# VectorE makes every addition of the softmax denominators in two attentions

## The chip, the cores and the metric

The kernel runs on one core of a Trainium2 chip. The metric is the time of one execution on the device in microseconds, as the median of several runs. The engines of the core run side by side, each with its own in-order queue, and meet at semaphores: TensorE (PE; its weight loads are PEld), VectorE (DVE), ScalarE (ACT), GpSimd (POOL) and SyncE (SP), which starts most of the transfers.

## What is computed

The reference is a residual network of four layers, each a cross-attention and a mixture of experts, on x of 2 x 512 x 256 with a context of 2 x 1024 x 256. The change touches the attentions of layers 0 and 1. Layer 0 has 16 heads of 64, keys and values from the context, and clips the scores; layer 1 has 8 heads of 64, keys and values from the context and from the latents themselves (1024 + 512 keys here), with no clip.

```python
# layer 0
attn = jnp.einsum('bhnd,bhsd->bhns', q, k) * scale
attn = jnp.clip(attn, -11.0, 11.0)
attn = jax.nn.softmax(attn, axis=-1)
out = jnp.einsum('bhns,bhsd->bhnd', attn, v)
# layer 1
k = jnp.concatenate([k_x, k_l], axis=2)
v = jnp.concatenate([v_x, v_l], axis=2)
sim = jnp.einsum('bhid,bhjd->bhij', q, k)
attn = jax.nn.softmax(sim, axis=-1)
out = jnp.einsum('bhij,bhjd->bhid', attn, v)
```

## The kernel before

One function writes the queue of each engine. An attention goes in steps; one step is one pair of heads of one batch entry: 16 steps in layer 0, 8 in layer 1 (`self.steps` in `Plan64`). In a step, `attend` runs over nk tiles of 128 keys, kt = 0 to nk - 1; nk is 8 in layer 0 and 12 in layer 1. For one tile:

- TensorE makes the scores of both heads, keys down and 512 queries across, into two banks of a ring of four (lines 661 and 662, in layer 1 also 664, which adds the negated row maximum).
- ScalarE takes the exponential of both, out of the banks, into a tile of 128 x 1024 (`slot`, line 948). Tile 0 of a step goes to an accumulator `SA`, of which there are two in turn; the others go to a ring of three buffers `PT`. A buffer is written again when tile kt - 3 was both weighted and added.
- In layer 0 VectorE clips the exponentials between exp(-11) and exp(11), in place (line 814).
- Two tiles later TensorE multiplies the tile with the values (`weigh`, line 646) into bank 4.
- The denominator: for kt = 1 to nk - 1 the tile is added to `SA` elementwise, 128 x 1024, in place. In `Plan64` a table `adds` says which engine makes which addition: VectorE those with kt % 4 == 3 (line 807), GpSimd the others (line 1009). Each waits for the one before it. Both engines issue add(kt - 2) in the iteration of tile kt, behind the clip of tile kt on VectorE, and the last two, add(nk - 2) and add(nk - 1), after the last tile's side work.

Between tiles a generator of side work is advanced by a number of turns worked out ahead (`paced`): first `divide` of the step before (line 680 on TensorE sums `SA` over the partitions with a matrix of ones and waits for the last addition; line 824 takes the reciprocal, line 827 multiplies bank 4 by it), then parts of `prepare` of the next step: projections of keys (line 275, `mm3`), the rotation (744 on VectorE, the sum 979 on GpSimd), the split of the keys into two parts (872 on ScalarE, 728 on VectorE), `output` (692, 837), values (572, 880, 884), and at the end the projection of the queries, which ScalarE places (907) and VectorE splits (765). The first scores of the next step wait for these (`placed`). In layer 1 the row maxima follow: line 624 makes scores for them, VectorE reduces them one by one (785), then over the parts with a negation (790), and ScalarE spreads that on a diagonal (925), for which the next step's scores wait. Every second step VectorE also splits the next weights (720), after ScalarE (866). What is left of the side work once the tiles are through is run before the next step; on VectorE that is behind the last two additions.

TensorE's `divide` stands in its queue behind the scores of the next step's tile 0, and ahead of the next key projection. In the last step of an attention there is nothing to prepare, and the side work is over after tile 0.

Of the kernel before, what the change touches and what calls it, by code (L numbers as in the profile page):

```python
# [33 lines left out]
class Semaphores(dict):  # L34


    def __init__(self, nc, ctx):
        super().__init__()
        self.nc, self.ctx = nc, ctx
# [105 lines left out]
def paced(weights, total, shares):  # L145

    out, done, i = [], 0.0, 0
    for share in shares:
        n = 0
        while done < share * total - 1e-6 and i < len(weights):  # L150
            done += weights[i]
            i += 1
            n += 1
        out.append(n)
    return out
# [6 lines left out]
class Kernel:  # L162
# [74 lines left out]
    def view(self, off, cnt, pat=None, **kw):  # L237
        v = self.AF[:, off:off + cnt]
        return v.rearrange(pat, **kw) if pat else v

    def rview(self, off, cnt, pat=None, **kw):
        v = self.AR[:, off:off + cnt]
        return v.rearrange(pat, **kw) if pat else v

    def pair(self, off, cnt, pat=None, **kw):
        return self.rview(off, cnt, pat, **kw), self.rview(off + cnt, cnt, pat, **kw)
# [226 lines left out]
class Plan64:  # L473


    def __init__(self, K, layer):
        self.own = layer == 1
        self.layer = layer
        S = 1536 if self.own else 1024
        self.nk = nk = S // P  # L480
        rview, view, pair = K.rview, K.view, K.pair
        self.KT = [rview(6144 + 3072 * i, 2 * S, "p (h n) -> p h n", h=2) for i in range(2)]
        self.QA = [rview(12288 + 2048 * i, 1024, "p (h n) -> p h n", h=2) for i in range(2)]
        self.QB = [rview(13312 + 2048 * i, 1024, "p (h n) -> p h n", h=2) for i in range(2)]
        self.DG = [rview(16384 + 1024 * i, 1024, "p (h n) -> p h n", h=2) for i in range(2)]
        self.PT = [view(5120 + 1024 * i, 1024, "p (h n) -> p h n", h=2) for i in range(3)]
        self.VA = [view(8192 + 1536 * i, nk * 128, "p (t c) -> p t c", c=128) for i in range(2)]
        self.OT, self.VT = view(11264, 512), view(11776, 512)
        self.COS, self.SIN = K.TB[:, 0:1024], K.TB[:, 1024:2048]
        self.W = [pair(4096, 1024), pair(18432, 1024)]  # L490
        self.SA = [view(15616 + 1024 * i, 1024, "p (h n) -> p h n", h=2) for i in range(2)]
        self.TM = [view(2048 + 1024 * i, 1024, "p (h n) -> p h n", h=2) for i in range(2)]
        self.npair = 4 if self.own else 8
        self.steps = [(p, b) for p in range(self.npair) for b in range(B)]
        self.n = len(self.steps)
        prep = [1.3] * 4 + [1.3, 0.4, 1.3, 0.4] + [1.3]
        if self.own:
            prep += [1.3, 1.3, 0.4] + [0.85] * 24 + [0.0]
        total = sum(prep) + 1.5
        shares = [(kt + 1) / nk for kt in range(nk)]  # L500
        self.pace = []
        for n in range(self.n):
            ahead = prep if n + 1 < self.n else [0.0, 0.0]
            weights = [0.5] * (n > 0) + ahead[:2] + [1.0] * (n > 0) + ahead[2:]
            self.pace.append(paced(weights, total, shares))

        self.k_lo = 6 if self.own else 4
        self.nv = 3 if self.own else 2

        self.adds, made = {}, K.adds_made  # L510
        for n in range(self.n):
            for kt in range(1, nk):
                who = "sum_vector" if kt % 4 == 3 else "sum_gpsimd"
                made[who] += 1
                self.adds[n, kt] = who, made[who]

# [195 lines left out]
def vector_attention64(v, K, A, bases):  # L712
    own, nk = A.own, A.nk
    wv0, ex0, o0 = (bases[x] for x in ("weighed", "exp", "out"))
# [84 lines left out]
    def add(n, kt):  # L799
        if kt < 1 or A.adds[n, kt][0] != "sum_vector":  # L800
            return
        if kt > 1:
            v.wait_ge(*A.adds[n, kt - 1])
        v.wait_ge("exp", ex0 + 2 * (n * nk + kt + 1))
        if not own:
            v.wait_ge("clip", bases["clip"] + n * nk + kt + 1)
        v.e.tensor_tensor(A.SA[n % 2], A.SA[n % 2], A.slot(n, kt), ALU.add).then_inc(*v.up("sum_vector"))  # L807

    def attend(n, side):
        for kt in range(nk):  # L810
            if not own:
                pt = A.slot(n, kt)
                v.wait_ge("exp", ex0 + 2 * (n * nk + kt + 1))
                v.e.tensor_scalar(pt, pt, CLIP_LO, CLIP_HI, ALU.max, ALU.min).then_inc(*v.up("clip"))  # L814
            add(n, kt - 2)
            run(side, A.pace[n][kt])
        add(n, nk - 2)
        add(n, nk - 1)
# [1828 lines left out]
```

## Time and profile before

| | |
|---|---|
| Time, median of 3 runs | 2950.0 us (2949.27 to 2957.69) |
| The profiled execution | 2951.47 us |
| Its span | 2949.7 us |
| Mean granted clock of TensorE | 0.883 |
| Busy, share of the span | PE 81%, PEld 57%, DVE 53%, ACT 31%, POOL 32% |
| First attention, steps | 90 to 605 us of the span |
| Second attention, steps | 910 to 1364 us |

The busy time of an engine counts what it executes, not what it waits for. A time in brackets behind an instruction of the timeline is the idle time of its engine ahead of it, with what ended it. The granted clock is 1.00 at 2.4 GHz and 0.50 at 1.2 GHz.

### The profile page before, as it was taken

The numbers are of one execution on the slowest core, as the hardware profiler recorded it, in microseconds if no ns is written. First come the engines' busy times: TensorE is split into PE (matmuls) and PEld (weight loads), VectorE is DVE, ScalarE is ACT, GpSimd is POOL, SyncE is SP. The second block draws the span as 40 slices with busy tenths as digits, with TensorE's granted clock in tenths as the row PEclk, the third lists the DMA queues.
The fourth block names the chain that finished last, engine by engine and source line by source line (L and its number), as shares of the span: only waits on it lengthen the run. The fifth ranks groups of instructions, "written<-read, shape, count | busy, mean of one in ns | idle before, by whom it ended". The sixth has DMA issues, their size and how long they took to land.

```text
span 2949.7 us, 31683 instructions
## 1 busy us (share of the span) xinstructions
PE 2375.2 (81%) x11832; PEld 1668.5 (57%) x11832; DVE 1576.8 (53%) x2705; ACT 907.5 (31%) x1752; POOL 948.3 (32%) x817
## 2 busy tenths in 40 slices
PE   3799999848968999996885777399788989659994
PEld 2455555528955555553874454289644444348884
DVE  5788888743145665653315766322477767421222
ACT  2454555412124444442112223000224444401111
POOL 2354554433332342333222211355400000044443
PEclk8899999959978999997897777599879999769997
DMA  3000000008930000000482321199522221048883
GB/s 119 1 9 10 18 10 10 1 33 310 316 128 1 0 10 9 1 1 15 157 273 71 80 65 50 48 318 327 164 57 69 59 62 45 17 170 298 300 296 116
DMA packets 103178, 298.08 MB, mean 101 GB/s; under 512 B 16913, under 2 KB 45841, under 8 KB 102641
## 3 DMA queue, kind: packets, MB, share of 16 engines
q0 software_dynamic: 45168, 206.99, 20.3%
q1 hardware_dynamic: 57856, 89.07, 10.2%
q8 instruction: 94, 1.54, 0.2%
q14 instruction: 60, 0.48, 0.1%
HBM read 244.22 MB, written 20.32 MB: 90 GB/s over the span
## 4 chain that ended last, share of the span: by engine, by line
PE 41%; DVE 12%; issue 7%; DMA 4%; POOL 2%; ACT 2%; SPq 0%; another core or an unknown queue 0%; DVEq 0%; POOLq 0%; ACTq 0%
PE psum L1860 8%; PE psum L275 7%; PE psum L1883 6%; PE psum L1211 3%; DVE plain L1363 3%; PE psum L1224 2%; PE psum L646 2%; DMA plain<-in_l_en,plain 2%; PE psum L1184 2%; PE psum L661 2%; DVE plain L1381 2%; DMA plain<-sorted_x 2%; DVE plain L1360 1%; PE psum L1250 1%; PE psum L664 1%
## 5 line engine op out<-in xcount | busy, mean ns | idle before, releaser
L275 PE MATMUL psum<-split 128*128 128x512 f32 (+1 forms) x1776 | 475.3, 416 | 57.1 <-DVE split L348 11.1
L1860 PE MATMUL psum<-plain 128*128 128x128 f32 x3904 | 494.4, 279 | 10.2 <-DMA plain<-in_l_shared 8.5
L1860 PEld LDWEIGHTS psum<-plain 128*128 128x128 f32 x3904 | 486.3, 196 | 22.3 <-issue 10.5
L275 PEld LDWEIGHTS psum<-split 128*128 128x128 f32 x1776 | 337.0, 208 | 191.8 <-issue 95.7
L1009 POOL TENSOR_TENSOR plain<-plain 128x1024 f32<-128x1024 f32 x144 | 363.5, 2524 | 239.8 <-DVE plain L807 195.9
L1984 POOL DMA_INDIRECT plain<-in_l_ffn,plain x274 | 259.8, 948 | 401.7 <-PE psum L1883 378.7
L948 ACT ACTIVATE plain<-psum 128x512 f32<-128x512 f32 x448 | 251.4, 595 | 310.5 <-PE psum L664 145.2
L1883 PE MATMUL psum<-plain 128*128 128x256 f32 x1160 | 304.2, 385 | 28.0 <-DVE plain L1949 25.5
L1480 ACT ACTIVATE plain<-psum 128x512 f32<-128x512 f32 (+3 forms) x384 | 185.8, 542 | 228.7 <-PE psum L1224 227.6
L646 PE MATMUL psum<-plain 128*64 128x512 f32 x896 | 236.9, 616 | 5.6 <-DVE plain L814 5.6
L1949 DVE TENSOR_TENSOR plain<-plain,psum 128x256 f32<-128x256 f32 x198 | 81.7, 419 | 298.2 <-ACT plain L1908 266.5
L1184 PE MATMUL psum<-split 128*128 128x512 f32 (+3 forms) x384 | 171.8, 517 | 75.6 <-DVE plain L1381 29.9
L1883 PEld LDWEIGHTS psum<-plain 128*128 128x128 f32 x1160 | 199.9, 192 | 49.9 <-DVE plain L1949 25.5
L1908 ACT ACTIVATE plain<-psum 128x256 f32<-128x256 f32 x198 | 75.8, 384 | 491.2 <-PE psum L1860 461.8
L661 PE MATMUL psum<-split 128*128 128x512 f32 x448 | 186.2, 416 | 39.2 <-issue 20.1
L662 PE MATMUL psum<-split 128*128 128x512 f32 x448 | 178.3, 398 | 0.0
L313 PE MATMUL psum<-plain 128*128 128x128 f32 x224 | 48.8, 395 | 157.4 <-DVE plain L303 121.1
L1363 DVE TENSOR_REDUCE plain<-psum 128x1 f32<-128x512 f32 x256 | 159.2, 684 | 29.0 <-PE psum L1184 28.4
L1184 PEld LDWEIGHTS psum<-split 128*128 128x128 f32 x384 | 87.1, 230 | 148.2 <-DVE plain L1363 47.6
L979 POOL TENSOR_TENSOR plain<-plain 128x512 f32<-128x512 f32 x44 | 60.7, 1380 | 342.1 <-DVE plain L744 312.7
L814 DVE TENSOR_SCALAR plain<-plain 128x1024 f32<-128x1024 f32 x128 | 136.1, 1063 | 57.6 <-ACT plain L948 57.0
L728 DVE TENSOR_TENSOR split<-plain,split 64x512 fp32r<-64x512 f32 x96 | 143.4, 1494 | 30.7 <-ACT split L872 27.4
(177 smaller groups left out, 3024.7 us busy)
## 6 DMA issues: line engine op xcount, KB each, us to landing
split<-split SPq DMA_DIRECT2D x288, 64.0 KB, 2.0
split<-split SPq DMA_DIRECT2D x96, 128.0 KB, 2.4
plain<-sorted_x SPq DMA_DIRECT2D x76, 128.0 KB
sorted_y<-plain SPq DMA_DIRECT2D x76, 128.0 KB
plain<-in_l_w SPq DMA_DIRECT2D x16, 512.0 KB
plain<-in_l_w SPq DMA_DIRECT2D x12, 640.0 KB, 3.8
plain<-in_l_ffn,plain POOLq DMA_INDIRECT x274
plain<-in_ctx SPq DMA_DIRECT2D x8, 512.0 KB, 6.1
```

The lines of the kernel that those rows point to most:

```text
L275: m = t.e.matmul(out, lhs[x], rhs[y], start=(first and n == 0), stop=(last and n == 2), skip_group_check=skip)
L646: m = t.e.matmul(K.bank(4)[64 * h:64 * h + 64, :], A.VA[i][:, kt, 64 * h:64 * h + 64], pt[:, h, :], start=(kt == 0), stop=(kt == nk - 1))
L661: t.e.matmul(K.bank(b), kk, A.QA[i][:, h, :], start=True, stop=False)
L662: m = t.e.matmul(K.bank(b), kk, A.QB[i][:, h, :], start=False, stop=not own)
L948: s.e.activation(pt[:, h, :], K.where("scores", k), ACT.Exp, scale=0.125).then_inc(*s.up("exp"))
L1009: g.e.tensor_tensor(A.SA[n % 2], A.SA[n % 2], A.slot(n, kt), ALU.add).then_inc(*g.up("sum_gpsimd"))
L1184: t.e.matmul(K.bank(b)[:, 0:kn], A.QZ[:, j, 128 * q:128 * q + 128], A.KHL[0][:, 512 * u:512 * u + kn], start=True, stop=True).then_inc(*t. ...
L1363: v.e.tensor_reduce(A.MXC[:, q, u:u + 1], s, AX.X, ALU.max).then_inc(*v.up("row_max", L, n, j, q, u))
L1480: s.e.activation(pt[:, j % 2, q0:512], K.bank(K.at.get(("scores", L, n, kt, j), 0))[:, q0:512], ACT.Exp, scale=0.25).then_inc(*s.up("exp", ...
L1860: m = t.e.matmul(K.bank(b)[:, 256 * z + P * f:256 * z + P * f + P], ws[:, f, c0:c0 + 128], xt[:, k, :], start=(f == 0 and k == 0 and z == ...
L1883: m = t.e.matmul(y, h[:, f, :], ws[:, f, A.cn - 256:A.cn], start=(u == 0 and f == 0), stop=(u == units - 1 and f == 1))
L1984: g.e.indirect_dma_start(A.W[A.slot(i)].rearrange("p f n -> p (f n)"), None, K.T[f"l{L}_ffn"], bass.IndirectOffsetOnAxis(K.WIX[:, j - A.ns ...
```

## The change

In `Plan64`, which plans both attentions, the table gives every addition to VectorE. The addition of tile 1 therefore is VectorE's now, and gets the wait that GpSimd's had: tile 0 lies in `SA`, and may be overwritten once it was weighted. Nothing else is changed: the place of each addition in the iteration is the same on both engines.

```diff
@@ -510,7 +510,7 @@
         self.adds, made = {}, K.adds_made
         for n in range(self.n):
             for kt in range(1, nk):
-                who = "sum_vector" if kt % 4 == 3 else "sum_gpsimd"
+                who = "sum_vector"
                 made[who] += 1
                 self.adds[n, kt] = who, made[who]
 
@@ -801,6 +801,9 @@
             return
         if kt > 1:
             v.wait_ge(*A.adds[n, kt - 1])
+        else:
+
+            v.wait_ge("weighed", wv0 + n * nk + 1)
         v.wait_ge("exp", ex0 + 2 * (n * nk + kt + 1))
         if not own:
             v.wait_ge("clip", bases["clip"] + n * nk + kt + 1)
```

## Rows read from the trace of the kernel before

**Rows 1.** Page's costliest groups: busy us, mean ns, idle before; then L807's durations.

```profile
L1009 POOL TENSOR_TENSOR plain<-plain 128x1024 f32<-128x1024 f32 x144 | 363.5, 2524 | 239.8 <-DVE plain L807 195.9
L814 DVE TENSOR_SCALAR plain<-plain 128x1024 f32<-128x1024 f32 x128 | 136.1, 1063 | 57.6 <-ACT plain L948 57.0
L728 DVE TENSOR_TENSOR split<-plain,split 64x512 fp32r<-64x512 f32 x96 | 143.4, 1494 | 30.7 <-ACT split L872 27.4
...
L807 DVE TENSOR_TENSOR plain<-plain x56: 1212/1222/1227, 113.4 to 1362.7; 128x1024 f32<-128x1024 f32 x56
...
L728 DVE TENSOR_TENSOR split<-plain,split x96: 685/689/2783, 38.2 to 1283.2; 64x512 fp32r<-64x512 f32 x96
```

**Rows 2.** Windows, two steps of the first attention: engines' busy us, granted clock.

```profile
187.48:219.64 32.16, 30.50 (x127) 17.36 (x126) 27.12 (x28) 16.98 (x29) 15.81 (x8) 1.00 0.00 1
219.64:251.48 31.84, 30.36 (x126) 17.35 (x126) 26.04 (x27) 15.92 (x28) 15.80 (x8) 1.00 0.06 21
```

**Rows 3.** Waits of TensorE, 100 to 550 us: total us, times, longest.

```profile
PE psum L661 <- issue: 18.7, 13, 1.4
PE psum L646 <- DVE plain L814: 3.0, 1, 3.0
```

**Rows 4.** Timeline across the end of one step: start, us, engine, line, [idle before].

```profile
216.03 2.13 DVE L814 TENSOR_SCALAR plain<-plain 128x1024 f32<-128x1024 f32 x1 [0.65 <-ACT plain L948]
...
217.80 2.44 ACT L907 ACTIVATE split<-psum 64x512 fp32r<-64x512 f32 x4 [1.81 <-PE psum L275]
...
220.28 0.69 DVE L765 TENSOR_TENSOR split<-psum,split 64x512 fp32r<-64x512 f32 x1 [0.55 <-ACT split L907]
221.00 1.23 DVE L807 TENSOR_TENSOR plain<-plain 128x1024 f32<-128x1024 f32 x1
...
221.07 0.47 PE L661 MATMUL psum<-split 128*128 128x512 f32 x1 [1.44 <-issue]
...
222.28 0.20 PEld L680 LDWEIGHTS psum<-plain 128*64 128x64 f32 x4 [0.48 <-DVE plain L807]
...
222.98 0.69 DVE L814 TENSOR_SCALAR plain<-plain 128x1024 f32<-128x1024 f32 x1 [0.76 <-ACT plain L948]
...
228.07 0.20 PEld L646 LDWEIGHTS psum<-plain 128*64 128x64 f32 x4 [0.35 <-DVE plain L827]
```

**Rows 5.** Timeline in the middle of two steps.

```profile
209.33 1.09 ACT L948 ACTIVATE plain<-psum 128x512 f32<-128x512 f32 x2 [0.88 <-POOL plain L1009]
...
232.02 2.94 DVE L728 TENSOR_TENSOR split<-plain,split 64x512 fp32r<-64x512 f32 x2 [0.29 <-ACT split L872]
```

**Rows 6.** Timeline at the end of the first attention's first step, VectorE and TensorE.

```profile
120.78 2.08 DVE L814 TENSOR_SCALAR plain<-plain 128x1024 f32<-128x1024 f32 x1 [0.41 <-ACT plain L948]
...
122.92 1.08 PE L646 MATMUL psum<-plain 128*64 128x512 f32 x4 [2.99 <-DVE plain L814]
123.92 0.70 PE L661 MATMUL psum<-split 128*128 128x512 f32 x1
...
127.63 1.65 PE L275 MATMUL psum<-split 128*128 128x512 f32 x6
```

**Rows 7.** Timeline in the first attention's last step.

```profile
589.09 1.36 DVE L814 TENSOR_SCALAR plain<-plain 128x1024 f32<-128x1024 f32 x1 [1.43 <-ACT plain L948]
...
603.71 1.23 DVE L807 TENSOR_TENSOR plain<-plain 128x1024 f32<-128x1024 f32 x1 [2.24 <-POOL plain L1009]
```

**Rows 8.** Timeline in the second attention: inside a step, and across its end.

```profile
1003.37 1.89 DVE L785 TENSOR_REDUCE plain<-psum 128x1 f32<-128x512 f32 x3 [1.41 <-PE psum L624]
...
1022.82 1.22 DVE L807 TENSOR_TENSOR plain<-plain 128x1024 f32<-128x1024 f32 x1
1023.95 0.16 DVE L790 TENSOR_REDUCE plain<-plain 128x4 f32<-128x12 f32 x1
...
1025.47 0.50 PE L661 MATMUL psum<-split 128*128 128x512 f32 x1 [2.16 <-ACT split L925]
```

**Rows 9.** Windows behind four of six such stalls: busy us, then the granted clock.

```profile
1025.40:1028.80 3.40, 3.33 (x13) 1.90 (x14) 0.61 (x1) 1.21 (x3) 0.00 (x0) 1.00 0.00 0
1086.60:1090.00 3.40, 3.40 (x9) 1.20 (x8) 0.97 (x1) 0.92 (x2) 0.00 (x0) 0.50 0.00 0
...
1265.80:1269.20 3.40, 3.40 (x13) 1.91 (x14) 0.69 (x1) 1.20 (x2) 0.00 (x0) 1.00 0.00 0
1325.50:1329.00 3.50, 2.17 (x5) 0.30 (x4) 1.28 (x1) 0.82 (x2) 0.00 (x0) 0.51 0.00 0
```

## What the change will do to the time

> **What bounds the kernel now.** Read the page first. The costliest group of GpSimd is the one the change removes, 144 additions of 2.52 us, and two groups of VectorE show a mean far above their shortest form: the clip L814 and the subtraction L728 [rows 1]. Then the busy time of two successive steps of the first attention: they take 32.16 and 31.84 us, TensorE is busy for 30.5 and 30.4 us of them at full clock, VectorE for 27.1 and 26.0, ScalarE and GpSimd for half [rows 2]. So TensorE sets the pace, VectorE is close behind. Then the waits of TensorE: in the stretch from 100 to 550 us nearly all its idle time is one stall of 1.44 us, once a step, ahead of the next step's first score matmul, and the profile names no releaser for it [rows 3]. The timeline names it [rows 4]: the query projection ends at 217.8, ScalarE places it in four pieces (L907, 2.44 us), VectorE subtracts (second L765, over at 220.97), and TensorE starts at 221.07. Anything that lengthens this chain, or adds a second stall to TensorE's in-order queue, is paid in full, 14 times (13 in that stretch, and once more at 573 us).
>
> **The change, part by part.** *Removed:* all 144 additions of GpSimd, 80 in the first attention (5 in each of 16 steps) and 64 in the second (8 in each of 8). *Added:* as many on VectorE, at 1.22 us, the time of its own additions of that shape, whose shortest and longest differ by 15 ns [rows 1]. That is 5 x 1.22 = 6.1 us a step in the first attention.
>
> *The relief.* Beside a GpSimd addition the clip takes 2.13 us, without one 0.69 [rows 4]; two L728 take 2.94 us beside one [rows 5], where the shortest of them takes 0.685 [rows 1]. With means of 1.06 and 1.49, eight clips and four L728 a step give back 8 x 0.37 + 4 x 0.80 = 6.2 us. VectorE's busy time stays where it is, 26 to 27 us a step. Which of these microseconds lie on the path decides the time, so I go by the order of the queues.
>
> *Inside a step.* VectorE's queue is clip(kt), add(kt-2), side work. The longest chain it makes: exp(kt) needs the buffer that add(kt-3) read, so exp, clip, add form a loop of 1.09 + 0.69 + 1.22 + about 0.05 = 3.05 us. Placed beside the trace of one step, exp(5) starts about 0.9 us earlier (GpSimd's add held it until 209.33 [rows 5]), exp(7) about 0.6 us later; the last clip, 1.44 us shorter, ends 0.8 us earlier, and add(5), queued ahead of the two L765, ends about 0.6 us before ScalarE has the first of them ready. The stall of 1.44 us stays: it hangs on L907, not on the adds or the clip. Cover left: 0.6 us. Nothing gained, nothing lost. The one new wait of VectorE, on the first weighting ahead of add(1), is for something done some 5 us earlier.
>
> *At the step's end.* add(6) and add(7) stand behind both L765. Before, GpSimd had done add(6) by then, and VectorE made only add(7), 221.00 to 222.23; L680, the matmul that sums over partitions, started at 222.28, already waiting for it [rows 4]. Now add(6) takes that place and add(7) follows, with 0.03 us for the wait on the one before. L680 starts 1.26 us later, and behind it in TensorE's queue stand the next projection and scores, with no slack before the next step's end. The reciprocal, the product and the first weighting at 228.07 move by no more than that [rows 4]. **14 x 1.26 = +17.6 us.** In every second step the weight split L720 follows the adds; it moves by the same 1.26 us and so does the projection that needs it.
>
> *The first of these transitions* is another case: TensorE waited 2.99 us for a clip of 2.08 us that now takes 0.69, and four scores and L680 ran at a lower clock, 3.71 us from 123.92 to 127.63 against the usual 2.22 [rows 6]. Clip at 121.47, three adds behind it (5, 6, 7) until 125.1, the split until 126.3, and the projection starts at 126.4 instead of 127.63. The reciprocal gains 0.9. I take **-1.0 us**.
>
> *The last step* has no side work after its first tile, and the loop of 3.05 us sets it. Clip 589.09 ends at 589.78 [rows 7], add(1) at 591.0, then exps every 3.05 us until 600.1, the last clip over at 601.9, three adds at 605.5. Before, the last addition, which waited for GpSimd, ended at 604.94 [rows 7]. **+0.6 us.**
>
> *The second attention.* Its steps are paced by the row maxima. In a tile VectorE is idle for 1.41 us between reductions [rows 8], and an add of 1.22 us without any wait fits in; cover left: 0.19 us a tile. If it didn't fit, TensorE would wait for a bank by the difference. At the step's end the negated maximum L790 is queued behind add(10) and add(11), of which GpSimd made the first: L807 at 1022.82, L790 at 1023.95, then ScalarE's L925, then TensorE after a stall of 2.16 us [rows 8]. One more add there: 6 x 1.25 = **+7.5 us** (of the seven transitions the first has its maximum ahead of the adds, and the last step waits for its exps).
>
> *TensorE's clock.* No row of before shows the longer stalls, so I bound them. Of the six stalls of 2.16 us, four were followed by some 3.4 us at half clock (1.2 GHz; granted 0.50, two rows of the four), two were not (1.00) [rows 9]; none of the fourteen of 1.44 us was (1.00 over both steps [rows 2]). The stall of 2.99 us was [rows 6]. The price of one is 3.71 - 2.22 = 1.5 us [rows 6]. In the second attention stalls grow to 3.4 us: I take six instead of four, 2 x 1.5 = +3.0 us. In the first attention a second stall of 1.26 us follows 1.2 us after that of 1.44: 2.7 us idle with work between. Between none and all 14 (0 to 21 us) I take four, nearer to the row of 1.44, as each stall alone is shorter than it: +6.0 us. The Trainium skill's "TensorE: Matmul & The Clock Gate" (The HAM clock gate) has just these two levels and says that idleness drops it; how much idleness in pieces is enough, these traces must tell.
>
> Sum: 17.6 - 1.0 + 0.6 + 7.5 + 3.0 + 6.0 = **+33.7 us** on the profiled execution's 2951.5 (its span of 2949.7 and 1.8 around it). The median of the runs is 2950.0, 1.5 below it: **2984 us**.
>
> **The rivals.** *A, forecast:* adds at the step's end are paid. *B, VectorE's busy time sets the time:* it is the busiest engine but TensorE and its busy time is left as it was, 6.1 added and 6.2 given back, so 2950 us. For it: the small margins. Against it: VectorE has 5 us of idle time a step, and the place of an instruction in its queue, not the sum, made L680 wait 0.48 us already [rows 4]. The Trainium skill's "Perfetto Trace Analysis" (Identifying the Most-Contended Engine) would look there, since it doesn't take matmul busy time as a measure; by that rule the change is neutral. *C, faster:* the step is paced by exps that GpSimd holds and clips that it stretches. If each step gained the 0.88 us of exp(5) [rows 5] and the 1.44 us of the last clip [rows 4], the first attention would gain 14 x (2.32 - 1.26) = 15 us; with the 7.5 us that the second attention costs that is 2943 us. It decides from the point at which L765 waits for VectorE and not for L907; the second L765 shows a wait of 0.55 us for L907 [rows 4], and the first one like it. The Trainium skill's "SBUF — State Buffer" (Who interferes with whom) lets a GpSimd instruction block VectorE for its whole length, and the 2.13 us agree, but it doesn't say that the path runs there. *D, far slower:* VectorE falls behind inside the step, its 0.6 us of cover gone. Each L765 later by x us adds 14x; with a late L979 or handoffs of 0.2 us in each turn of the loop x is 1: 2998 us, and all 14 drops of the clock in the first attention give 2999 by themselves.
>
> **How the numbers follow.** A 0.82, B 0.06, C 0.04, D 0.08. The lower end is the sum with no clock cost but for a missized first transition and last step: 2950 + 24.7 - 4 = 2970; the upper, eight or nine more drops of the clock at 1.5 us each, or part of D, 2997. Within 0.3% (what a measurement of this kernel can tell from no change) is 2941 to 2959. So C is the chance of faster, 0.04, B that of the same, 0.06, and A with D that of slower, 0.90.
>
> **What would show it.** L807 200 times at 1.22 us, no L1009; L814 near 0.7 us and L728 at 0.69; L680 2.5 us after a step's first score instead of 1.2; steps of 33.1 and 33.4 us; the stall ahead of it still 1.44 us; in the second attention stalls of 3.4 us. It is wrong if L680 doesn't wait for a second add, if L765 starts later than L907 allows, or if TensorE shows idle time in the middle of a step.

## The result

The changed kernel takes 2999.15 us (median of 4 runs, 2992.31 to 3003.92), the kernel before 2949.64 beside it: the ratio is 1.0161, with an interval of 1.0133 to 1.0189. That is 49.5 us slower, where 34 were forecast and 47 were the end of the range. A second measurement, below, gives 1.0158. The profiled execution is the slowest of the four, 3003.92 us with a span of 3002.2, so its time is 52.5 us over that of the profile of before.

The page after, its first line and three of its groups; they answer to [rows 1]:

```profile
PE 2395.7 (80%) x11832; PEld 1681.7 (56%) x11832; DVE 1629.4 (54%) x2849; ACT 907.0 (30%) x1752; POOL 583.2 (19%) x673
...
L810 DVE TENSOR_TENSOR plain<-plain 128x1024 f32<-128x1024 f32 x200 | 243.7, 1219 | 16.0 <-ACT plain L951 10.7
...
L982 POOL TENSOR_TENSOR plain<-plain 128x512 f32<-128x512 f32 x44 | 58.6, 1333 | 860.9 <-DVE plain L744 824.1
...
L817 DVE TENSOR_SCALAR plain<-plain 128x1024 f32<-128x1024 f32 x128 | 95.9, 749 | 85.3 <-ACT plain L951 84.8
```

GpSimd has lost 365 us of busy time, VectorE has gained 53: 144 additions of 1.22 us, less what its other instructions no longer lose to GpSimd. The clip, L817 now, went from a mean of 1.06 to 0.75 us. The subtraction L728 now never takes more than 0.69 us, as its line's own view shows (shortest, median, longest):

```profile
L728 DVE TENSOR_TENSOR split<-plain,split x96: 684/687/690, 38.9 to 1326.6; 64x512 fp32r<-64x512 f32 x96
```

The end of a step in the timeline after, against [rows 4]; behind each line in brackets is its engine's idle time and what ended it:

```profile
224.58 2.44 ACT L910 ACTIVATE split<-psum 64x512 fp32r<-64x512 f32 x4 [1.38 <-PE psum L275]
...
227.05 0.69 DVE L765 TENSOR_TENSOR split<-psum,split 64x512 fp32r<-64x512 f32 x1 [0.55 <-ACT split L910]
227.78 2.48 DVE L810 TENSOR_TENSOR plain<-plain 128x1024 f32<-128x1024 f32 x2
227.84 0.47 PE L661 MATMUL psum<-split 128*128 128x512 f32 x1 [1.44 <-issue]
...
230.31 1.08 PE L680 MATMUL psum<-plain 128*64 128x512 f32 x4 [1.30 <-DVE plain L810]
231.32 1.65 PE L275 MATMUL psum<-split 128*128 128x512 f32 x6
```

The stall of 1.44 us is where it was, with the same chain behind it. Two additions stand behind L765 instead of one, and L680 starts 2.47 us after the step's first score where it started 1.21 after it. In the second attention the stall ahead of a step's scores grew from 2.16 to 3.42 us, as two additions stand ahead of the negated maximum L790, against [rows 8]:

```profile
1056.93 2.47 DVE L810 TENSOR_TENSOR plain<-plain 128x1024 f32<-128x1024 f32 x2
1059.33 0.16 DVE L790 TENSOR_REDUCE plain<-plain 128x4 f32<-128x12 f32 x1
...
1060.85 0.76 PE L661 MATMUL psum<-split 128*128 128x512 f32 x1 [3.42 <-ACT split L928]
```

What differs most from the forecast is TensorE's clock. A drop means below that the granted clock falls from 1.00 (2.4 GHz) to 0.50 (1.2 GHz). Windows after, two steps of the first attention and then pieces of the first of them (busy us of PE, PEld, DVE, ACT, POOL, then the granted clock):

```profile
192.08:227.84 35.76, 33.02 (x126) 18.96 (x127) 27.76 (x33) 16.23 (x29) 2.55 (x2) 0.90 0.00 1
227.84:261.17 33.33, 30.51 (x126) 17.35 (x127) 25.94 (x32) 16.66 (x29) 2.86 (x2) 1.00 0.07 20
...
193.90:197.20 3.30, 2.65 (x6) 0.94 (x7) 2.96 (x4) 0.06 (x1) 0.00 (x0) 0.50 0.02 5
197.30:200.60 3.30, 3.30 (x9) 2.54 (x9) 3.27 (x3) 0.24 (x1) 0.00 (x0) 0.50 0.00 0
200.80:201.00 0.20, 0.20 (x2) 0.17 (x1) 0.20 (x1) 0.15 (x1) 0.00 (x0) 1.00 0.00 0
```

One step is at 2.4 GHz throughout and takes 33.3 us, as forecast. The other starts at 192.08, is at 1.2 GHz from some 194.0, before the end of the stall at L680, until 200.8, some 6.8 us, and takes 35.8 us. That is twice as long as behind the stall of 2.99 us in [rows 6], as these windows of before show:

```profile
120.50:124.00 3.50, 1.08 (x5) 0.27 (x5) 3.12 (x2) 1.30 (x2) 1.81 (x1) 1.00 0.00 0
124.10:127.40 3.30, 3.30 (x8) 1.19 (x8) 1.92 (x3) 1.19 (x2) 0.00 (x0) 0.50 0.02 5
127.50:130.00 2.50, 2.50 (x12) 1.99 (x11) 2.25 (x1) 0.14 (x1) 0.00 (x0) 1.00 0.00 0
```

Six of the thirteen steps between 157 and 603 us have a drop and are 34.9 to 35.9 us long; in five of them it lasts 6.8 us, in one, the shortest, 3.4. The other seven take 32.9 to 33.5 us.

### The profile page after: what moved, and what is told of

It is laid out like the page before. It is cut to its first block, busy times and chain, and to the rows that moved or that the text cites. A ratio compares the mean times of both kernels' runs of the same rounds, so it can differ in the third digit from the quotient of the medians.

```text
span 3002.2 us, 31683 instructions
## 1 busy us (share of the span) xinstructions
PE 2395.7 (80%) x11832; PEld 1681.7 (56%) x11832; DVE 1629.4 (54%) x2849; ACT 907.0 (30%) x1752; POOL 583.2 (19%) x673
## 3 DMA queue, kind: packets, MB, share of 16 engines
q0 software_dynamic: 45168, 206.99, 19.8%
q1 hardware_dynamic: 57856, 89.07, 10.1%
## 4 chain that ended last, share of the span: by engine, by line
PE 40%; DVE 13%; DMA 5%; issue 4%; POOL 3%; ACT 2%; SPq 0%; POOLq 0%; DVEq 0%; ACTq 0%
PE psum L1863 7%; PE psum L275 7%; PE psum L1886 5%; PE psum L1214 3%; DVE plain L1366 3%; PE psum L1227 2%; DMA plain<-in_l_en,plain 2%; PE psum L646 2%; PE psum L1187 2%; DVE plain L1384 2%; DMA plain<-sorted_x 2%; PE psum L661 1%; PE psum L1253 1%; DVE plain L1363 1%; PE psum L664 1%
## 5 line engine op out<-in xcount | busy, mean ns | idle before, releaser
L275 PE MATMUL psum<-split 128*128 128x512 f32 (+1 forms) x1776 | 484.9, 422 | 53.1 <-DVE split L348 11.1
L275 PEld LDWEIGHTS psum<-split 128*128 128x128 f32 x1776 | 344.3, 212 | 195.7 <-issue 96.0
L810 DVE TENSOR_TENSOR plain<-plain 128x1024 f32<-128x1024 f32 x200 | 243.7, 1219 | 16.0 <-ACT plain L951 10.7
L646 PE MATMUL psum<-plain 128*64 128x512 f32 x896 | 236.7, 615 | 4.6 <-DVE plain L817 4.6
L1187 PEld LDWEIGHTS psum<-split 128*128 128x128 f32 x384 | 87.5, 231 | 147.8 <-DVE plain L1366 47.6
L661 PEld LDWEIGHTS psum<-split 128*128 128x128 f32 x448 | 87.5, 195 | 102.7 <-issue 34.5
L817 DVE TENSOR_SCALAR plain<-plain 128x1024 f32<-128x1024 f32 x128 | 95.9, 749 | 85.3 <-ACT plain L951 84.8
```

What stands on the lines that cost most here:

```text
L275: m = t.e.matmul(out, lhs[x], rhs[y], start=(first and n == 0), stop=(last and n == 2), skip_group_check=skip)
L646: m = t.e.matmul(K.bank(4)[64 * h:64 * h + 64, :], A.VA[i][:, kt, 64 * h:64 * h + 64], pt[:, h, :], start=(kt == 0), stop=(kt == nk - 1))
L661: t.e.matmul(K.bank(b), kk, A.QA[i][:, h, :], start=True, stop=False)
L1187: t.e.matmul(K.bank(b)[:, 0:kn], A.QZ[:, j, 128 * q:128 * q + 128], A.KHL[0][:, 512 * u:512 * u + kn], start=True, stop=True).then_inc(*t. ...
```

## Experiments

All are measured against the kernel before on the same chip; it took 2957 to 2960 us there as a median, so ratios are compared, not microseconds.

To take the stages apart I use one pair of stretches in every profile. The first runs from the first reciprocal of the first attention (L824 before, L827 after) to the fifteenth, which are the 14 steps with the stall of 1.44 us; the second from the first to the seventh reciprocal of the second attention, 6 steps. Before, and then after:

```profile
127.76:575.86 448.10, 425.85 (x1764) 242.86 (x1764) 371.56 (x370) 229.43 (x398) 221.21 (x98) 1.00 0.03 9
969.90:1327.70 357.80, 332.47 (x1332) 194.30 (x1332) 219.09 (x284) 159.05 (x290) 131.69 (x60) 0.98 0.01 4
```

```profile
127.84:606.94 479.10, 439.65 (x1763) 251.06 (x1762) 374.30 (x441) 228.86 (x398) 38.20 (x28) 0.96 0.03 9
1004.00:1374.40 370.40, 337.53 (x1332) 196.60 (x1332) 252.05 (x332) 159.07 (x290) 15.29 (x12) 0.96 0.01 4
```

So 31.0 us of the 52.5 are in the first stretch and 12.6 in the second. VectorE's busy time in the first is 374.3 against 371.6 us: 70 more additions there cost it 2.7 us net.

### One attention at a time

```diff
-                who = "sum_vector"
+                who = "sum_vector" if layer == 0 or kt % 4 == 3 else "sum_gpsimd"
```

> The change in the first attention alone. Theory: 14 stalls of 1.31 us (18.3 us) and some 6 drops of the clock at 2.5 us (15 us), so 33 us, 2979 to 2986 us. Rival (what was missing in the forecast arose outside the first attention): 18.3 + 6, 2974 us.

Measured: 1.0093 (1.0062 to 1.0124), 27.5 us. The first stretch takes 478.8 us, as in the changed kernel. The same with `layer == 1`:

> The change in the second attention alone. Theory: 6 stalls longer by 1.26 us (7.6 us) and 2 to 4 more drops of the clock at 1.5 to 2.5 us, so 11 to 15 us, 2961 to 2965 us. Rival (the clock costs nothing there): 2957 us.

Measured: 1.0047 (1.0030 to 1.0063), 13.9 us. The second stretch takes 370.6 us, as in the changed kernel. The two add up to 41 us against the 47 of the whole (1.0158); the interval of the first alone is 9 us to either side. The first is 5 us below what was expected of it, so its total doesn't tell the two cases apart, while its stretch does: the 31 us are inside it. The second, with at least 8.9 us by its interval, is above the 7.6 us of the longer stalls alone.

### The last but one addition back on GpSimd

```diff
-                who = "sum_vector"
+                who = "sum_gpsimd" if kt == nk - 2 else "sum_vector"
```

> VectorE makes all additions but the last but one of each step, add(nk - 2), which GpSimd makes. Theory (place in the queue, and the clock that its stall costs): L680 starts 1.2 us after a step's first score as in the kernel before, the second attention's stall is 2.16 us again, steps of 31.8 and 32.2 us with a granted clock of 1.00; with about 1 us more in each attention's last step 2948 to 2955 us. Rival (the load moved to VectorE inside the steps, 4 of the 5 additions, costs by itself): most of the 49.5 us stays, above 2985 us.

Measured: 1.0009 (0.9993 to 1.0025). VectorE makes 120 of the 144 moved additions and the time is that of before. Its two stretches take 449.3 and 359.3 us, at clocks of 1.00 and 0.99. Only the second attention's stall was missed: it is 2.56 us and not 2.16, since GpSimd, 2.36 us for its addition, makes VectorE wait 0.31 us for it. The load that was moved costs nothing inside the steps; the rival falls.

### The stalls filled

The changed kernel, with matmuls whose result is overwritten by what follows in the same bank. They are issued while TensorE would stand still. `own` is true in the second attention.

```diff
     def divide(n):
...
+        if n + 1 < A.n and not own:
+            i = (n + 1) % 2
+            for _ in range(5):
+                t.e.matmul(K.bank(b), A.KT[i][:, 0, 0:128], A.QA[i][:, 0, :], start=True, stop=True)
         t.wait_ge(*A.adds[n, nk - 1])
...
     def attend(n, side):
         i = n % 2
+        if n:
+            b = RS.banks[RS.n % len(RS.banks)]
+            t.bank(b)
+            for _ in range(12 if own else 5):
+                t.e.matmul(K.bank(b), A.KT[1 - i][:, 0, 0:128], A.QA[1 - i][:, 0, :], start=True, stop=True)
         placed(n)
```

> The changed kernel with matmuls of no use (their result is overwritten) in the stalls of TensorE: 5 ahead of a step's first scores and 5 ahead of L680 in the first attention, 12 ahead of a step's first scores in the second. They take 0.23 us each and fit into the stalls of 1.44, 1.31 and 3.42 us. Theory: order costs 26 us, the clock the rest; with the stalls filled the granted clock is 1.00 in all steps and of the first attention's steps none is longer than 33.5 us: 2999 less 14 to 20, 2978 to 2986 us. Rival (the clock falls for another reason than idleness at the step's end, or the time is lost elsewhere): 2996 us or more.

Measured: 1.0083 (1.0047 to 1.0119), against 1.0158 without the matmuls: 22 us less, with more work on TensorE and the same waits. Its two stretches:

```profile
127.16:591.46 464.30, 459.90 (x1904) 268.19 (x1904) 370.22 (x440) 228.51 (x398) 40.14 (x28) 1.00 0.03 9
990.40:1350.70 360.30, 345.03 (x1404) 204.88 (x1404) 252.00 (x333) 159.10 (x290) 15.30 (x12) 1.00 0.01 4
```

The granted clock is 1.00 in both. The order of the queue alone costs 464.3 - 448.1 = 16.2 us in the first; what the clock adds there is 479.1 - 464.3 = 14.8 us. This is the experiment that separates the two terms: nothing but the idleness of TensorE was changed. Its steps take 32.9 to 33.5 us, which is what the seven steps without a drop take in the changed kernel.

The control is the kernel before with the second half of this edit, 8 matmuls in place of 12:

> The kernel before with 5 matmuls of no use ahead of a step's first scores in the first attention and 8 in the second, in the stalls of 1.44 and 2.16 us. Theory: in the first attention nothing changes (no drop there behind a stall of 1.44), in the second the drops behind 2.16 us go, 3 to 4 x 1.5 us: ratio 0.998 to 0.999. Rival (the matmuls of no use cost time themselves, so that the filled version of the changed kernel understated the clock): above 1.001.

Measured: 1.0003 (0.9986 to 1.0021), no difference. In the stretches both halves of the expectation hold: 448.5 us in the first, as without the matmuls, and 352.7 in the second, 5.1 less than before.

```profile
975.60:1328.30 352.70, 339.45 (x1380) 200.32 (x1380) 218.99 (x285) 159.08 (x290) 131.71 (x60) 1.00 0.01 4
```

The gain does not show in the total. Code that no version touches, from the last reciprocal of the second attention (the eighth) on, took between 1574.7 and 1588.8 us in thirteen profiles; 5 us are lost in that. By these rows the second attention's order costs 360.3 - 352.7 = 7.6 us, its clock 5.1 us before and 10.1 after.

### One tile earlier

```diff
-            add(n, kt - 2)
+            add(n, kt - 1)
             run(side, A.pace[n][kt])
-        add(n, nk - 2)
         add(n, nk - 1)
```

> All additions on VectorE as in the changed kernel, but add(kt - 1) instead of add(kt - 2) in the iteration of tile kt, so that one addition and not two stands behind the side work at a step's end. Same work, same engine. Theory (place in the queue): L680 starts 1.2 us after a step's first score, no drop of the clock in the first attention, second attention's stalls 2.16 us, and the first attention's last step 1 to 2 us shorter than before: ratio to the kernel before 0.998 to 1.000. Rival (the load on VectorE costs, wherever it stands): the 49.5 us stay, 1.016.

Measured: 1.0098 (1.0079 to 1.0117). That is 29 us where none was expected, and the rival would have had 47. The first stretch takes 478.8 us with a granted clock of 1.00, so neither L680 nor the clock is to blame. The timeline names the place; L839 is the addition of the output to x (L837 before), L810 the addition:

```profile
197.71 1.08 PE L646 MATMUL psum<-plain 128*64 128x512 f32 x4
...
199.85 2.28 DVE L810 TENSOR_TENSOR plain<-plain 128x1024 f32<-128x1024 f32 x1
...
202.06 1.62 DVE L839 TENSOR_TENSOR plain<-plain,psum 128x256 f32<-128x256 f32 x4
202.52 0.70 PE L692 MATMUL psum<-plain 128*128 128x256 f32 x2 [2.24 <-DVE plain L839]
```

add(1) now stands ahead of L839, which empties the banks that TensorE needs for L692, and it takes 2.28 us there instead of 1.22, beside GpSimd's L981, which runs from 199.47 to 201.05. The weighting that it needs (L646 of 197.71) is over by then, so it is not that wait. TensorE stands for some 2.2 us in each of the 14 steps, 30.8 us in all. The cost went from one place in VectorE's queue to another. What the move was meant for did come: L680 follows 1.2 us after the first score, and the last step is 4.9 us shorter (32.8 us between the fifteenth and sixteenth reciprocals, 37.7 before). With the second attention's maximum first as well:

```diff
+        if own and n + 1 < A.n:
+            run(side, 1000)
         add(n, nk - 1)
```

> As the one before, and in the second attention the rest of the side work, with the negated maximum L790, runs ahead of the last addition of a step (but for the last step). Theory: its stalls fall from 2.16 to about 0.95 us, 6 x 1.2 = 7 us, and the clock's drops behind them go, some 3 x 1.5 us: ratio 0.994 to 0.997, so faster than both kernels. Rival (TensorE then waits for the addition at L680 instead): 0.999.

Measured: 1.0069 (1.0044 to 1.0094). The first stretch is as without this edit (478.8 us), so the ratio expected was out of reach; the second takes 346.6 us instead of 356.9, and its stalls are 1.16 us long. And with matmuls of no use ahead of a step's first scores, 5 in the first attention and 4 in the second:

> As the one before, with 5 matmuls of no use ahead of a step's first scores in the first attention and 4 in the second, inside the stalls of 1.44 and 0.95 us. Theory: nothing is left to save at these stalls, since the clock stays at 1.00 with such stalls anyway: same as the one before within 2 us. Rival (short stalls cost clock too): 5 us or more less.

Measured: 1.0084 (1.0068 to 1.0099), not faster. The matmuls save nothing at stalls this short: the second stretch takes 346.5 us, as without them. The first takes 485.4 us instead of 478.8. Its last four steps took 35.7 us instead of 34.2, each with a drop of 3.4 us that begins within some 1.5 us of the end of its stall of 2.2 us at L692 (two of the four):

```profile
480.00:483.40 3.40, 3.40 (x10) 2.07 (x10) 1.96 (x3) 0.96 (x2) 0.00 (x0) 0.51 0.00 0
585.90:589.30 3.40, 3.38 (x8) 2.72 (x9) 2.41 (x5) 0.00 (x0) 0.00 (x0) 0.50 0.02 5
```

All 14 steps have that stall. Why the clock fell in these four and not in the other ten was not settled.

### Caught up in the middle of the step

```diff
-            add(n, kt - 2)
+            if kt < catch:
+                add(n, kt - 2)
+            elif kt == catch:
+                add(n, kt - 2)
+                add(n, kt - 1)
+            else:
+                add(n, kt - 1)
             run(side, A.pace[n][kt])
-        add(n, nk - 2)
         add(n, nk - 1)
```

Here `catch` is 6 in the first attention and 4 in the second.

> All additions on VectorE. The lag is two tiles as in the changed kernel up to tile 6 of a step in the first attention and tile 4 in the second, where two additions are made, and one tile after that. So add(1) isn't issued before the first weighting it waits for, and only one addition stands at the step's end. Theory (only the place in the queue costs): steps of 31.8 and 32.2 us, no stall at L692 as with the lag of one, no drop of the clock in the first attention: ratio to the kernel before 0.998 to 1.001. Rival (VectorE's load has to be paid somewhere in the step, and each place taken from it shows up in another): steps of 33 us or more, ratio 1.006 or above.

Measured: 0.9999 (0.9988 to 1.0010). The first stretch:

```profile
124.58:572.58 448.00, 425.48 (x1763) 242.56 (x1762) 368.85 (x440) 228.47 (x398) 40.16 (x28) 1.00 0.03 10
```

448.0 us against 448.1 before, with all additions on VectorE. The 47 us are gone by issuing additions one tile earlier within the same queue, two in a step of the first attention (add(5) and add(6)) and eight in a step of the second, so that one less stands at the step's end. With the maximum first:

> As the one before, and in the second attention L790 ahead of the last addition. Theory: stalls of 1.16 instead of 2.16 us there and no drops of the clock behind them, 9 to 11 us less than the kernel before: ratio 0.995 to 0.998, faster than both. Rival: 1.000.

Measured: 0.9959 (0.9945 to 0.9974), 2947.4 us against 2957.2: faster than the kernel before by 10 us (12 by the ratio) and so than both. Its first stretch takes 448.2 us; the second, and the end of one of its steps:

```profile
967.30:1314.00 346.70, 327.37 (x1332) 191.81 (x1332) 252.76 (x332) 159.10 (x290) 15.31 (x12) 1.00 0.01 4
```

```profile
1020.37 0.17 DVE L790 TENSOR_REDUCE plain<-plain 128x4 f32<-128x12 f32 x1
1020.45 1.22 DVE L810 TENSOR_TENSOR plain<-plain 128x1024 f32<-128x1024 f32 x1
...
1021.90 0.50 PE L661 MATMUL psum<-split 128*128 128x512 f32 x1 [1.16 <-ACT split L937]
```

The maximum is ahead of the addition, the stall is 1.16 us where [rows 8] had 2.16, and the stretch is 11.1 us shorter than before: 6 x 1.0 from the stall and 5.1 from the clock, which is now 1.00. The gain is that of the maximum's place and not of the additions' engine, since without it the ratio is 0.9999. What the same move would give with the additions left on GpSimd was not run.

### The changed kernel again

> The changed kernel itself once more, on the same chip and in the same job as the two above, for their ratios and for the seven or so drops of the clock in the first attention in another execution: 1.016, and 5 to 8 of 14 steps with part of them at half clock.

Measured: 1.0158 (1.0139 to 1.0177). Its first stretch takes 475.0 us at a clock of 0.97, its second 370.7: in another execution the clock cost 10.7 us (475.0 - 464.3) and not 14.8 in the first attention. It has four drops there, one fewer than the least expected, and each lasts 6.8 us:

```profile
222.50:229.30 6.80, 6.05 (x14) 3.61 (x15) 5.29 (x5) 0.40 (x2) 0.00 (x0) 0.50 0.00 0
324.90:331.70 6.80, 6.12 (x14) 3.68 (x15) 6.43 (x6) 0.41 (x2) 0.00 (x0) 0.50 0.00 0
427.30:434.10 6.80, 5.97 (x14) 3.50 (x15) 5.29 (x4) 0.41 (x2) 0.00 (x0) 0.50 0.00 0
529.70:536.50 6.80, 6.26 (x14) 3.78 (x15) 6.43 (x6) 0.45 (x1) 0.00 (x0) 0.50 0.01 2
```

So a drop cost 2.7 us here. What the clock costs changes from one execution to the next; the steps without a drop take 32.9 to 33.5 us in both.

## Why the prediction was wrong

The direction, the place and the order of the queue were right. The term that failed is TensorE's clock, and the range missed the median by 2 us. Point by point, in the profiled execution:

- *L680 behind a second addition, forecast 17.6 us.* Right: the stall is 1.30 us long and the term is 16.2 us.
- *The chain L907 to L765 sets the stall of 1.44 us, and the relief gains nothing.* Right. The stall is 1.44 us in all steps, and VectorE's busy time moved by 2.7 us of 372.
- *Cover of 0.6 us ahead of L765.* Right in size: its first instance shows a wait of 0.76 us for ScalarE.
- *The first transition, -1.0 us.* Right in sign, too large: the first reciprocal comes 34.0 us after the first clip, 34.3 before.
- *The last step, +0.6 us.* Between the last two reciprocals of the first attention it is 1.2 us in this profile and 0.2 in the one taken again.
- *The second attention's order, 7.5 us.* Right: 7.6 us, and stalls of 3.42 us. The 0.19 us of cover in each tile held.
- *TensorE's clock, +9.0 us in all.* This step failed. I took four drops at 1.5 us for the first attention, nearer to the row of the stall of 1.44 us, because neither of the two stalls is longer than it. Six long steps gave 14.8 us, some 2.5 us each, for in five of them the clock stayed low for 6.8 us, twice as long as after the stall that the price was read from. In the other execution there were just the four drops forecast, and they cost 10.7 us instead of 6.0. So the price of a drop was too low in both, and the number in one. The pair of stalls, 2.7 us idle around 1.2 us of work, dropped the clock in six steps, where the stall of 1.44 us alone never did; the stall of 1.30 us alone was not run, and why a drop lasts 3.4 us in one step and 6.8 in another stays open. In the second attention all six steps dropped, as forecast, at a net 5.0 us instead of 3.0. Together 19.8 us for 9.0: that is 10.8 of the 18.8 us by which the profiled execution exceeds the forecast's sum, and with them the forecast would have been 2995 us. The Trainium skill's "TensorE: Matmul & The Clock Gate" (The HAM clock gate) has the drop behind an idle stretch; these runs show it behind a pair of short ones too.
- *Outside both stretches.* 31.0 and 12.6 us leave 8.9 of 52.5: 1.2 in the last step, 1.9 from there to the second stretch, 5.7 behind them, and 0.1 ahead. The forecast had no term for the 1.9 and the 5.7. The 5.7 lie inside the spread of 1574.7 to 1588.8 us that this untouched code shows over thirteen profiles. No run tells whether the change has a part in it; as a median the kernel is 3 us closer to the forecast than in its profile.

Of the rivals, B (the sum of VectorE's busy time sets the time) is refuted: the changed kernel has 31 us in its first stretch at 2.7 us more of that busy time; the kernel that catches up in the middle of a step makes the same additions on the same engine without the 47 us; the one with the lag of one tile has 30 us in another place. C (faster) didn't occur, and L765 still waits for ScalarE. D's mechanism inside the step, VectorE behind by 1 us, didn't occur either. Its other half, a larger loss to the clock than taken, is the larger part of the difference. The upper end of the range should have been that of all drops, 2999, and at 2.5 us a drop instead of 1.5 it would have been higher still.

## What to carry to other kernels

Price work that moves between engines by where it lands in the receiving engine's in-order queue, not only by what it adds to its busy time: look for what stands behind each instruction moved. Here a second addition ahead of L680 cost 16.2 us, one ahead of L839 30.7, and the same additions in the middle of the step nothing. When a new stall falls close to an old one, allow for a loss to the clock as large as the stalls' own (14.8 us beside 16.2 here); bound it by every step, and by a longer drop than the one that a trace happens to show. Matmuls into a bank that is about to be overwritten, put into the stalls, tell how much of a loss is the clock's. Here they also took 22 us off the changed kernel, and nothing where the stall was one of 1.44 us alone.

## What the runs showed of the hardware

- Two stalls of 1.44 and 1.30 us with 1.2 us of work between brought TensorE to 1.2 GHz in six of thirteen steps, in five for 6.8 us, and in another execution in four, each for 6.8 us; a single stall of 1.44 us in none of fourteen. Stalls of 1.44 and 2.24 us with some ten microseconds of work between left the clock at 1.00 over 14 steps in two profiles. With the stall of 1.44 us filled, the one of 2.2 us had 3.4 us at 1.2 GHz at or just behind its end in four of 14 steps.
- An addition of 128x1024 takes GpSimd 2.36 to 2.87 us and VectorE 1.22. Beside GpSimd's, a subtraction of 64x512 on VectorE took up to 2.78 us; with those gone, at most 0.69 in 96 instances.
